# One VectorE subtraction moved behind the q part of the next step, in a fused chain of cross attention, self attention and MLPs

## The reference, cut to what matters

```python
def _attn(xq, xc, Wq, Wk, Wv, Wo, bo):
    q = (xq @ Wq).reshape(B, N, HEADS, D_HEAD)      # 16 heads of 64, N = 512
    k = (xc @ Wk).reshape(B, S, HEADS, D_HEAD)
    v = (xc @ Wv).reshape(B, S, HEADS, D_HEAD)
    scores = jnp.einsum('bnhd,bshd->bhns', q, k) * D_HEAD ** (-0.5)
    attn = jax.nn.softmax(scores, axis=-1)
    out = jnp.einsum('bhns,bshd->bnhd', attn, v).reshape(B, N, HEADS * D_HEAD)
    return out @ Wo + bo
...
x = _attn(_ln(x, g1, b1), _ln(x, g1, b1), Wq1, Wk1, Wv1, Wo1, bo1) + x
```

## Time and profile before

| | us |
|---|---|
| median of 3 runs | 2230.24 |
| lowest and highest of them | 2229.74, 2231.28 |
| the profiled execution | 2229.74 |
| its span, first to last instruction | 2228.0 |
| busy: PE, DVE, ACT, POOL | 2097.6, 1580.5, 1486.8, 1018.0 |

### The profile page before, as it was taken

One profiled execution on the slowest core, in us unless ns is written; L12 is line 12 of the kernel. 1 busy time (PEld: TensorE's weight loads), 2 busy tenths in 40 slices (PEclk: granted clock), 3 DMA queues, 4 the chain that ended last, 5 costly groups with the idle time before them and its releaser, 6 DMA issues. The chain is left out here.

```text
span 2228.0 us, 31299 instructions
## 1 busy us (share of the span) xinstructions
PE 2097.6 (94%) x11628; PEld 1775.7 (80%) x11628; DVE 1580.5 (71%) x2349; ACT 1486.8 (67%) x2157; POOL 1018.0 (46%) x830
## 2 busy tenths in 40 slices
PE   6868999998899999999999999999997799999998
PEld 4657888887788888888788888887876689898887
DVE  5566776665787777877778778787785866666543
ACT  5546788766777777777777777777773355455431
POOL 3155454440354354454534445445454666655422
PEclk9978999999999999999999999999998899999999
DMA  6910000021000100101001010010004411111000
GB/s 202 318 45 6 22 22 22 11 70 47 21 25 15 34 15 15 39 16 34 15 16 34 15 35 16 19 34 15 25 27 180 149 39 57 41 55 48 10 10 20
DMA packets 84280, 102.67 MB, mean 46 GB/s; under 512 B 29664, under 2 KB 61152, under 8 KB 83616
## 3 DMA queue, kind: packets, MB, share of 16 engines
q1 hardware_dynamic: 84128, 100.66, 13.7%
HBM read 65.50 MB, written 33.82 MB: 45 GB/s over the span
## 5 line engine op out<-in xcount | busy, mean ns | idle before, releaser
L146 PE MATMUL PS<-R 128*128 128x256 f32 (+1 forms) x2944 | 1024.5, 348 | 69.6 <-DVE R L162 24.4
L148 PE MATMUL PS<-R 128*128 128x256 f32 (+1 forms) x2944 | 994.3, 338 | 0.0
L147 PE MATMUL PS<-R 128*128 128x256 f32 (+1 forms) x2944 | 994.0, 338 | 0.0
L146 PEld LDWEIGHTS PS<-R 128*128 128x128 f32 x2944 | 562.2, 191 | 186.2 <-issue 47.5
L156 ACT ACTIVATE R<-PS 64x512 fp32r<-64x512 f32 (+4 forms) x860 | 459.6, 547 | 257.3 <-PE PS L1833 131.0
L148 PEld LDWEIGHTS PS<-R 128*128 128x128 f32 x2944 | 561.5, 191 | 60.4
L147 PEld LDWEIGHTS PS<-R 128*128 128x128 f32 x2944 | 562.7, 191 | 54.7
L162 DVE TENSOR_TENSOR R<-F,R 128x1024 fp32r<-128x1024 f32 (+2 forms) x418 | 436.5, 1058 | 37.0 <-POOL R L159 22.1
L159 POOL TENSOR_SCALAR R<-F 128x512 fp32r<-128x512 f32 (+1 forms) x293 | 305.1, 1043 | 185.4 <-DVE F L1990 147.5
L1618 DVE TENSOR_REDUCE F<-PS 128x2 f32<-128x1024 f32 x256 | 301.4, 1215 | 10.8 <-PE PS L1421 10.8
L162 DVE TENSOR_TENSOR R<-PS,R 128x512 fp32r<-128x512 f32 (+3 forms) x348 | 180.8, 542 | 176.4 <-ACT R L156 175.7
(11 more groups left out here) (92 smaller groups left out, 2003.5 us busy)
## 6 DMA issues: line engine op xcount, KB each, us to landing
F<-sd SPq DMA_DIRECT2D x128, 128.0 KB, 2.9
xs<-F SPq DMA_DIRECT2D x16, 512.0 KB, 3.6
F<-xs SPq DMA_DIRECT2D x16, 512.0 KB, 3.5
gd<-F SPq DMA_DIRECT2D x8, 768.0 KB, 4.4
vd<-F SPq DMA_DIRECT2D x8, 768.0 KB, 6.8
R<-gd SPq DMA_DIRECT2D x6, 1024.0 KB, 5.6
R<-vd SPq DMA_DIRECT2D x6, 1024.0 KB, 5.7
F<-in_x SPq DMA_DIRECT2D x8, 512.0 KB, 5.2
```

Source lines behind the costliest of these rows:

```text
L146: nc.tensor.matmul(o, L[0], Rr[0], start=start, stop=False, skip_group_check=share)
L147: nc.tensor.matmul(o, L[0], Rr[1], start=False, stop=False, skip_group_check=share)
L148: return nc.tensor.matmul(o, L[1], Rr[0], start=False, stop=stop, skip_group_check=share)
```

## The change

In `dve_attention1`, the call that makes the low part of the last quarter of the step before, `rests(4 * s - 1)`, moves down by two blocks of code: behind the subtractions of q and the reciprocal, ahead of the subtractions of k. Nothing else differs.

```diff
                 for j in range(4):
-                    if j == 0:
-                        rests(4 * s - 1)
                     if ok(u, N3) and j == 0:
                         project(u, 0)
                     if ok(d - 1, N3) and j == 0:
                         k, i = (d - 1) % 2, (d - 1) // 2
                         dve.wait_ge(sum3[k], 2 * i + 1)
                         dve.wait_ge(out3[k], i - 1)
                         nc.vector.reciprocal(SR3[k], SQ3[k]).then_inc(rec3.sem, 1)
+                    if j == 0:
+                        rests(4 * s - 1)
                     if ok(u, N3) and j == 0:
                         project(u, 1)
```

## The result

The changed kernel takes 2247.89 us (median of 4 runs, 2247.59 to 2248.10) against 2229.99 (4 runs, 2229.45 to 2231.28): a ratio of 1.0080, 95% interval 1.0061 to 1.0097. It is slower, as forecast, but by 18 us and not by 90, and it lies 2 us under the lower end of the range. The profiled execution took 2249.57 us, its span is 2247.8.

A forecast was written before the change was run, and what follows sets the result against it. PE bounds, with little in hand. 22 even steps x 1.86, 28 odd x 1.11 and 7 norm x 1.22 give 80.5 us, the seven others 10: 90.5 on 2229.7, so 2320 us (+4.1%), range 2250 to 2345.

The forecast's parts named there:

- Point 1: VectorE's k subtractions run 1015.10 to 1016.51, and PE's load for the first score product goes from 1015.90 to 1016.56.
- point 2: ScalarE's second exponential waits for the moved subtraction (1015.28, not 1014.07); VectorE's v subtraction, behind its v copies, is 1.21 late.
- The rooms of the two maxima: Even step, slack of VectorE's maxima before PE's loads: 0.34 for quarter 0, 0.12 for quarter 2.
- that of k: Even step, slack between VectorE's end of the k low parts and PE's load for the first score product: 0.77.
- Point 4: GpSimd's copy, no longer beside a VectorE subtraction, falls from 1.54 to 0.62; its subtraction starts at 1020.71, not 1021.52.
- Where it lands: Part on the new place, ahead of the k subtractions: GpSimd's two 64-partition copies delay the moved subtraction, ending at 1015.19.
- the choice of one copy: The moved subtraction waits for one of GpSimd's two 64-partition copies: 1013.50 + 0.61 + 1.08 = 1015.19.
- a wait for both: Moved subtraction waits for both GpSimd copies, ending 1015.81; as a rival 0.62 later every step, 2360 us, chance 0.06.
- whoever comes second waits: Rule for VectorE's two-SBUF-input subtractions beside GpSimd operations, from a trace where one took 2.00 in place of 1.22.
- point 5: VectorE's quarter-1 subtraction finds GpSimd's running, ending 1023.07, not 1022.18; PE's output load goes to 1024.25, even step +1.86.
- the first rival: VectorE's quarter-1 subtraction gets in before GpSimd's: even steps +0.97, odd +0.29, 2273 us; chance 0.18.
- no lock costs anything: Rival: moved subtraction never meets GpSimd, ends 1014.89; all 0.91 late, even +0.67, norm +0.91, 2254 us; chance 0.10.

The follow-up runs named there:

- the kernel with v ahead: Changed kernel with ScalarE's two v copies moved ahead of its second exponential: 2240.33 us, 1.0046.
- The kernel with 0.28 more on VectorE: Changed kernel with an unused VectorE maximum over 256 columns of SBUF ahead of the moved subtraction: 2306.41 us, 1.0337.
- the one with 0.14 more: Changed kernel with two idle VectorE reciprocals of 8 columns ahead of the moved subtraction: 2264.94 us, 1.0153.
- the kernel with the maximum over 1024 columns: Kernel before, subtraction in its old place, with an unused VectorE maximum over 1024 SBUF columns where it had been moved: 2242.67 us, 1.0054.

## Why the prediction was right and wrong
**Right: what the move costs, and whom.** The old place was free: q and the reciprocal stand where they stood. Point 1 held (k and PE's first load late), and so did point 2: the second exponential waits for VectorE, 0.78, and v hangs on it, with the gap of 0.26 that the kernel with v ahead closes. The rooms of the two maxima were right to a hundredth, that of k to 0.08. VectorE's results are 0.76 late in the even step; less the 0.12 of the maximum of quarter 2, and less the 0.12 that a stalled PE gets back, that leaves 0.52, and the step grew by 0.52. In the odd step the 0.61 that GpSimd had cost absorbs it: 17.83 before and after. In the norm step, without room, it is 0.75. Point 4 held too: GpSimd's copy is free (0.62) and its subtraction ready at +7.14 (forecast +7.25).

**Wrong: "Where it lands".** The step that failed is the choice of one copy, put between no cost and a wait for both. The forecast had GpSimd's copy, started first, holding the moved subtraction until +1.73. It ended at +1.28, and the kernel whose copies wait for it gives the same time: the right term was that range's lower end, no cost. I took the rule "whoever comes second waits" from the product in the earlier trace rows, with a lead of 0.38, and applied it to a lead that my own sum put at 0.17 and that the trace shows at 0.06. VectorE moreover started 0.11 behind the reciprocal, not 0.21 as the k subtraction did in the earlier trace rows, and took 1.17, not 1.22. All is 0.76 late instead of 1.21.

**Wrong in consequence: point 5.** 0.45 us earlier, VectorE reaches the quarter-1 subtraction at +7.05, 0.09 ahead of GpSimd, and the collision, 0.89 in the forecast's even step (1.86 less the 0.97 of the first rival), turns round: GpSimd is blocked, which delays no one but in the 7 steps of the 2.6 us. That collision was 47 of the 90 us (2320 less 2273). The kernel with 0.28 more on VectorE has it, at 19.04 a step and 75 us in all; the one with 0.14 more has it in some steps. The balance that the first rival named (a gap of 0.25, within the error of my chain) was thus real, but that rival kept the 1.21; what happened is the rival in which no lock costs anything, 2254 by its sum. Its even +0.67 and norm +0.91 came out as +0.52 and +0.75, for the 0.15 that VectorE's start and length were better than the row that I took them from. Steps add up to 17.4 of the 19.8 between the two spans. What lies ahead of and behind these 57 steps has both signs; the largest piece is +2.8 in the last step, where the moved subtraction stands behind a reciprocal that waits 5.0 us for a transfer (3.8 before).

**The chances.** The forecast had 0.57, no lock 0.10 and VectorE first 0.18. All three hang on one question, who gets the port, and the evidence for it was a single pair of rows with leads of 0.38 and a queued operation. The range left out the case that came true by 2 us.

By the Trainium skill (SBUF — State Buffer, "Who interferes with whom") an instruction with two SBUF inputs on VectorE contends with a GpSimd instruction that reads SBUF, and a reduction doesn't. The runs agree with both: 2.29 for the pair of copies beside the subtraction, 1.23 beside the maximum. Its further rule, that issue order decides who blocks, doesn't fit the order of recorded starts: copies recorded 0.06 to 0.47 ahead were the ones blocked.

## What to carry to other kernels
Where two engines share a port and start within some tenths of a microsecond of each other, don't settle who goes first by the recorded starts: work out the sum for both orders, and follow each to the next meeting, since 0.28 us at the first decided 57 us here. Where a chain is nearly as long as the one that bounds, the odd steps here, a delay elsewhere hides in it, and shortening that chain is the cheaper gain: here by a copy that went to ScalarE, which is busier than GpSimd in all (1486.8 against 1018.0) but doesn't meet VectorE's subtraction. A small dummy operation that shifts one engine by tenths shows how near a schedule stands to such a jump. It can also bring a meeting of its own, as the copy at +6.80 did, so the steps it makes have to be read before its total is taken for a cost.

## What the runs showed of the hardware
- Behind the reciprocal (a 0.19 us instruction) a subtraction with two SBUF inputs starts 0.11 later, where the k subtraction, with a PSUM input, started 0.21 later. A maximum of SBUF starts 0.11 later too.
- A blocked copy of GpSimd ends 0.47 to 0.48 after VectorE's subtraction; a blocked subtraction of VectorE ends 1.07 to 1.09 after GpSimd's operation. These ends tell who waited, even where the starts don't.
- Open: when does an earlier GpSimd operation get the port? Behind the reciprocal or a short maximum of SBUF VectorE always won, with copies 0.06 to 0.47 ahead. Behind a long maximum of PSUM it lost, with a lead of 0.38 in the earlier trace rows, of 0.03 to 0.11 in the kernel with two reciprocals (at 0.02 or less it won) and of 0.07 to 0.41 to the copy in the kernel with the maximum over 1024 columns, and in the kernel before also to a plain copy that had followed 4.68 us of idle time:
```profile
579.19 1.05 POOL L159 TENSOR_SCALAR R<-F 128x1024 fp32r<-128x1024 f32 x1 [4.68 <-PE PS L148]
...
579.28 3.16 DVE L162 TENSOR_TENSOR R<-F,R 128x1024 fp32r<-128x1024 f32 x2
```
  With 3.16 for two subtractions that otherwise take 2.35, the first one was held, by a lead of 0.09. So neither the lead, nor the kind of GpSimd's operation, nor its height decides. What VectorE does just before is one thing that differs; a run with a maximum of PSUM behind the reciprocal would test it, and wasn't made.
